# Feed-forward layer 1 by Strassen-Winograd block products, with low halves formed on GpSimd, in a fused two-layer attention kernel

## What is computed

```python
xn3 = _ln(x, g3, be3)                                   # 4096 tokens x 512
ff = jax.nn.relu(xn3 @ Wf1 + bf1) @ Wf2 + bf2           # Wf1 512 x 2048, Wf2 2048 x 512
return x + ff
# layer 1 then needs, per token row, x @ (folded Wt, Wg) + gb, a softmax over tokens,
# a sigmoid gate, and a layer norm
```

## Time and profile before

| | |
|---|---|
| median of 3 runs | 2268.39 us (2266.43 to 2272.82) |
| the profiled execution | 2266.88 us, of which its span is 2265.1 us |
| mean granted TensorE clock | 0.986 |
| busy, share of the span | PE 95%, PE weight load 71%, DVE 60%, ACT 42%, POOL 37% |
| chain that ended last | PE 83%, DVE 7%, ACT 5%, issue 2%, DMA 2%, POOL 1% |
| DMA | 177.35 MB, mean 78 GB/s |

### The profile page before, as it was taken

The page is one execution under the profiler, slowest core; times in us unless marked ns, Lnnn a source line. Parts: engine busy times, 40 slices in busy tenths (PEclk is TensorE's granted clock), DMA queues, the critical chain, the costliest instruction groups (busy, mean ns, idle before and its releaser), DMA issues.

```text
span 2265.1 us, 32190 instructions
## 1 busy us (share of the span) xinstructions
PE 2160.6 (95%) x11590; PEld 1602.6 (71%) x11590; DVE 1356.7 (60%) x3277; ACT 942.5 (42%) x1738; POOL 848.5 (37%) x887
## 2 busy tenths in 40 slices
PE   7999999999999998889999998999999999999996
PEld 5666666666656664467777776888887887888784
DVE  5577766776786667456666676442345536454536
ACT  4155655655565555534433344422322322232223
POOL 1068767777777778653333331000000000000002
PEclk9999999999999998899999999999999999999998
DMA  7655555565564455211111221320111221111101
GB/s 235 78 82 96 95 83 86 102 92 81 91 117 78 77 96 131 71 56 57 57 61 67 84 80 43 121 79 29 61 61 66 70 75 61 66 61 65 43 29 51
DMA packets 106324, 177.35 MB, mean 78 GB/s; under 512 B 18334, under 2 KB 23454, under 8 KB 106160
## 3 DMA queue, kind: packets, MB, share of 16 engines
q1 hardware_dynamic: 106164, 175.29, 33.6%
HBM read 83.67 MB, written 40.13 MB: 55 GB/s over the span
## 4 chain that ended last, share of the span: by engine, by line
PE 83%; DVE 7%; ACT 5%; issue 2%; DMA 2%; POOL 1%; SPq 0%; POOLq 0%; ACTq 0%; DVEq 0%
PE psum L55 20%; PE psum L56 19%; PE psum L57 19%; PE psum L830 6%; PE psum L775 6%; PE psum L818 5%; PE psum L733 1%; DVE psum L1036 1%; PE psum L839 1%; ACT sx L1386 1%; PE psum L1336 1%; PE psum L752 1%; DMA small<-es 1%; PE psum L1328 1%; PE psum L1277 1%
## 5 line engine op out<-in xcount | busy, mean ns | idle before, releaser
L690 POOL TENSOR_TENSOR es<-es,er 128x512 f32<-128x512 f32 (+3 forms) x640 | 587.5, 959 | 258.0 <-PE psum L830 242.9
L931 ACT ACTIVATE er<-psum 128x512 f32<-128x512 f32 (+3 forms) x640 | 278.4, 471 | 285.7 <-DVE psum L1047 178.5
L1036 DVE CUSTOM_DVE_ANT_0 psum<-psum,mask_ts 128x384 f32<-128x384 f32 (+3 forms) x512 | 249.0, 501 | 152.7 <-PE psum L775 150.3
L775 PE MATMUL psum<-ks,qs 96*128 96x512 f32 (+3 forms) x768 | 259.6, 370 | 7.2 <-DVE mx L1036 3.1
L818 PE MATMUL psum<-qs,ks 100*128 100x512 f32 (+3 forms) x768 | 251.3, 364 | 10.7 <-DVE mx L1036 5.4
L1874 ACT ACTIVATE fy<-psum,cols 128x512 f32<-128x512 f32 x128 | 88.2, 689 | 404.9 <-PE psum L57 404.3
L1982 DVE TENSOR_TENSOR hl<-fy,hh 128x512 fp32r<-128x512 f32 x128 | 89.5, 700 | 272.9 <-PE psum L57 195.2
L775 PEld LDWEIGHTS psum<-ks,qs 96*128 96x128 f32 x768 | 139.3, 190 | 115.4 <-issue 32.7
L1040 DVE TENSOR_REDUCE mx<-psum 128x1 fp32r<-128x512 f32 x256 | 175.4, 685 | 61.2 <-PE psum L775 60.3
L55 PE MATMUL psum<-fh,hh 128*128 128x512 f32 x512 | 201.0, 393 | 3.8 <-DVE hl L1982 3.5
L55 PE MATMUL psum<-fah,fh 128*128 128x512 f32 x512 | 203.2, 397 | 0.0
(11 more groups left out here) (260 smaller groups left out, 4539.3 us busy)
## 6 DMA issues: line engine op xcount, KB each, us to landing
qs<-stage SPq DMA_DIRECT2D x96, 256.0 KB, 5.7
ks<-stage SPq DMA_DIRECT2D x96, 256.0 KB, 8.3
rs<-rs_d SPq DMA_DIRECT2D x32, 256.0 KB
sa_d<-rs SPq DMA_DIRECT2D x32, 256.0 KB, 2.1
sx<-sa_d SPq DMA_DIRECT2D x8, 1024.0 KB, 5.8
xt<-in_x SPq DMA_DIRECT2D x32, 256.0 KB, 6.0
x_d<-xt SPq DMA_DIRECT2D x32, 256.0 KB, 2.0
fw<-in_Wf SPq DMA_DIRECT2D x16, 512.0 KB, 5.3
```

The source lines that it names most:

```text
L690: e.tensor_tensor(es, es, er, ALU.add).then_inc(s_add.sem, 1)
L775: t = e.matmul(bank1(*s)[:, v * wd:v * wd + wd], Q.qs[par][0:96, i, 128 * ti:128 * ti + 128], Q.ks[par][0:96, i, c0:c0 + wd], start=True, ...
L931: e.activation(dst, bank1("sc", g, c2, j, i)[:, off:512], ACT.Exp, scale=SCALE).then_inc(s_freeS.sem, 1)
L1036: t = e.tensor_tensor_reduce(out=ps, in0=ps, in1=mask_ts[:, 512 - wd:512], scale=1.0, scalar=-3e38, op0=ALU.add, op1=ALU.max, accum_out=mx ...
```

## The change

The first layer's product for two hidden tiles (256 units) and a chunk of 512 tokens is a 2x2 block product: the weights as a11, a12, a21, a22 (128 units x 256 inputs), the turned rows as b11 to b22 (256 inputs x 256 tokens). Instead of eight block products it forms seven, after Strassen and Winograd. A chunk is 8 such blocks `u`.

- Step `P(c, u, j)`, j = 0 to 6, replaces two `h` steps: 2 contraction blocks x 3 = 6 matmuls with 256 moving columns, so 42 a block, into four half-used banks A, B, C, D. `cp` (ACT) copies product 0 to SBUF (`cu`), and seven `pd` (DVE, 128x256, one operand in PSUM each) combine the products. Tile 2u is complete in bank A after `pd` 3, tile 2u+1 in bank D after `pd` 6.
- Sums of the turned rows: `tt`, four 128x512 subtractions on POOL. High halves of the seven right operands: `bh` (ACT, 7 a chunk); low halves `bl` (DVE, 7 a chunk, two SBUF operands). They replace the 4 copies and 4 subtractions of `cTl`.
- Sums of the weights, once, in chunk 0: `ws`, four 128x256 steps on POOL a block; `wa` 3 high halves on ACT, `wl` 3 low halves on DVE. `wo` writes the block of seven (high and low, 1.8 MB) to DRAM, and from chunk 1 on `wi` reads it back each time, 56 loads into three rotating buffers.
- `hs`, the low half of the relu output, moves from DVE to POOL. Its buffer `fy` is now single (`fr`), `hh` and `hl` have three buffers instead of two.
- The order: a block of TensorE work is 15 slots, `oPPoPPoPPoooPoo`; `o` is split by token tile, and the tiles of block u are consumed in block u+1. All nominal times of the stage are new. Before the seam's end only block 0's seven products stand, where three `h` stood.

```diff
+SLOTS = "oPPoPPoPPoooPoo"
+ADDED_AT = ((1, 2.66), (3, 1.23), (3, 2.65), (5, 1.02), (5, 0.38), (6, 1.29), (6, 1.32))
+HALVES_AT = ((5, 1.55, 2.54, 1.87), (6, 2.6, 2.4, 3.25))
...
+FF_ROWS = (-9.3, -6.31, -3.49, -7.61, -6.54, -5.7)
+FF_TURN = (-2, 0.07, 0.16, 0.01)
+FF_COMBINE = -3.32
...
+            elif s[0] == "wi":
+                n = s[1]
+                u = n % 8
+                w.wait_ge(s_prod, 7 * (n - 2))
...
+                e.dma_start(F.w1[n % 3][:].rearrange("p r a k n -> p (r a k n)").bitcast(F32), w1_d[u]).then_inc(d_wi[n % 3].sem, 16)
...
+            elif s[0] == "hs":
+                _, c, m = s
+                n = 16 * c + m
+                w.wait_ge(s_r3, n + 1)
+                w.wait_ge(s_hh3, n + 1)
...
+                e.tensor_tensor(F.hl[n % 3][:], F.yb[:], F.hh[n % 3][:].bitcast(F32), ALU.subtract).then_inc(s_h3.sem, 1)
+            elif s[0] == "tt":
+                c = s[1]
...
+                w.wait_ge(s_y3, 4 * c + 4)
+                e.tensor_tensor(t1, b12, b11, ALU.subtract).then_inc(s_tt.sem, 1)
+                w.wait_ge(s_tt, 4 * c + 1)
+                e.tensor_tensor(t2, b22, t1, ALU.subtract).then_inc(s_tt.sem, 1)
+                e.tensor_tensor(t3, b22, b12, ALU.subtract).then_inc(s_tt.sem, 1)
+                w.wait_ge(s_tt, 4 * c + 2)
+                e.tensor_tensor(t4, b21, t2, ALU.subtract).then_inc(s_tt.sem, 1)
...
-            elif s[0] == "h":
...
+            elif s[0] == "P":
...
+                wh, wl = (F.w1[n % 3][:, r, LEFT[j]] for r in range(2))
+                for k in range(2):
+                    t = three(e, bk, (wh[:, k, :], wl[:, k, :]), (F.bh[:, j, k, :], F.bl[:, j, k, :]), k == 0, k == 1)
+                t.then_inc(s_prod.sem, 1)
...
+            elif s[0] == "bl":
+                _, c, j = s
+                w.wait_ge(s_bh, 7 * c + j + 1)
+                e.tensor_tensor(F.bl[:, j], quarter(c, RIGHT[j]), F.bh[:, j].bitcast(F32), ALU.subtract).then_inc(s_x3.sem, 1)
+            elif s[0] == "pd":
...
+                w.wait_ge(s_prod, 7 * n + (2, 4, 4, 6, 6, 7, 7)[q])
+                w.wait_ge(s_pd, 7 * n + (0, 0, 2, 3, 3, 3, 5)[q])
...
+                e.tensor_tensor(o, x, y, ALU.add).then_inc(s_pd.sem, 1)
```

More of the change, by code:

```diff
@@ L289, in pre3 @@
     for k in range(KT):
[L290 to L304, removed]
@@ L305 @@
-FF_ROUTE = (35.7, 0, 0.1, 1.3, 1.5, 1.8, 3, 0.2)
-FF_LAST = (3.3, 3.6, -1.2)
-FF_TILE = (0, 0.2, 0.4, 0.8, 0.85, 1, 1.4, 1.6)
-def order3():
-    rows, turn, gate = FF_ROWS, FF_TURN, FF_GATE
-    t = [(n - 2.2 + a, (s, n)) for n in range(4, 16) for a, s in ((-0.01, "wd"), (0, "w"))] + [(15, ("w4",)), (1.81, ("wv",))]
+        t += [(FIRST_TURN[0] + FIRST_TURN[1] * k + a, (s, 0, k)) for a, s in ((0, "cT"), (FIRST_TURN[2], "cTh"))]
+    t.append((FIRST_TURN[3], ("tt", 0)))
+    for j in range(7):
+        a = FIRST_HALVES[0] + FIRST_HALVES[1] * j
+        t += [(a, ("bh", 0, j)), (a + FIRST_HALVES[2], ("bl", 0, j))]
@@ new lines @@
+FF_TILE = (0.05, 0.12, 0.4, 0.8, 1.02, 1.27, 1.86, 1.77)
+FF_WEIGHT = (-3.13, -2.44, -2.12, -1.61, -0.9, -2.72, -0.21)
+FF_END = 2.44
+def order3():
+    rows, turn, ready, slot = FF_ROWS, FF_TURN, FF_WEIGHT, BLOCK / 15
+    t = [(15, ("w4",)), (1.81, ("wv",))]
+    for u in range(8):
+        B = BLOCK * u
+        t += [(B + ready[0], ("wd", 2 * u)), (B + ready[5], ("wd", 2 * u + 1)), (B + ready[6], ("w", 2 * u + 1))]
+        t += [(B + a, (s, u)) for a, s in zip(ready[1:5], ("ws", "wa", "wl", "wo"))]
+    for n in range(8, 64):
+        t.append((BLOCK * (n - 2) + 0.05, ("wi", n)))
@@ new lines, in program @@
+            F.w1 = [block3(0)]
+            F.jk = sb(ctx, "jk", [128, C])
+            F.w2 += [half3(2), half3(3)]
+            with ExitStack() as early:
+                y0 = sb(early, "fy0", [128, KT, 512])
+            F.hh = [sb(ctx, f"hh{p}", [128, 512], F32R) for p in range(3)]
+            F.hl = [sb(ctx, f"hl{p}", [128, 512], F32R) for p in range(3)]
+            F.bh, F.bl = (sb(ctx, f"fa{j}", [128, 7, 2, 256], F32R) for j in "hl")
+            F.xt = [sb(ctx, "fx1", [128, 4, C])]
+            F.w1.append(block3(1))
@@ new lines, in program @@
+            F.wvb = sb(ctx, "wvb", [128, C])
+            F.w1.append(block3(2))
+            F.gb = sb(ctx, "gb", [128, C])
+            F.w2 += [half3(u) for u in range(4, 8)]
+            xn1 = sb(ctx, "fn", [128, 4, C])
+            F.xt.insert(0, sb(ctx, "fx0", [128, 4, C]))
+            with ExitStack() as early:
+                y1 = sb(early, "fy1", [128, KT, 512])
+            F.th, F.tl = [sb(ctx, f"th{i}", [128, KT, 128], F32R) for i in range(2)], [sb(ctx, f"tl{i}", [128, KT, 128], F32R) for i in range(2)]
@@ L1813, in pe3 @@
+                if m == 0 and c:
+                    w.wait_ge(s_o3, 4 * (c - 1) + i + 1)
+                elif m == 0 and i == 0:
+                    w.wait_ge(s_sub, 32)
+                elif m == 0:
+                    freeT(w, tail + i - 1)
+                r = slice(128 * i, 128 * i + 128)
+                three(e, acc[i], (F.hh[p][:, r], F.hl[p][:, r]), (f2h[:, m % 2, :], f2l[:, m % 2, :]),
+                      m == 0, m == 15).then_inc(s_out3.sem, 1)
             elif s[0] == "gT":
```

390 lines of the change are left out of this document (248 added, 142 removed).

## The result

The changed kernel takes 2354.33 us (median of 4 runs, 2349.65 to 2358.05) beside 2270.61 us for the kernel before on the same chip: ratio 1.0367, 95% interval 1.0348 to 1.0386. The prediction said 2262, range 2240 to 2284. The profiled execution has a span of 2356.3 us and a mean granted clock of 0.969 (0.986 before).

A forecast was written before the change was run, and what follows sets the result against it. TensorE was taken as the bound: matmul count times interval, plus waits. -25.2 - 6 + 18.8 + 3 + 2 + 2 = -5.4 us on the median 2268.4 gave 2263, put at 2262 for overlapping stalls; range 2240 to 2284.

The forecast's parts named there:

- The products: Feed-forward on TensorE: seven narrower products a block take 5.00 us instead of 5.44, a gain of 25.2 us (23 to 28).
- The old waits: TensorE's 7.4 us of waits before `gT` and `o` steps should mostly go: a gain of 6 us (0 to 7.4).
- The chain of tile 2u: From product 5 to the next block's first `o`: 3.40 us needed of 4.11, slack 0.71; no wait in a plain block.
- Rival 3: Slower, chance 0.23: tile 2u's low half misses its slot; 2281 us if in a third of the blocks, 2290 in half.
- The move of `hs` to POOL costs nothing by engine shares: 128 `hs` steps go to idle POOL: free by engine shares, but not by the port lock shared with DVE.
- Block 6: Chunks 0 to 6: `bx` on DVE and `tt` on POOL take turns, delaying `pd`; a loss of 18.8 us (0 to 28).
- `bl` at 1.5 us: Sign to look for: DVE's low halves `bl`, like `bx`, lengthened to 1.5 us beside `tt` and `hs` on POOL.
- The `e` steps: Blocks 3 to 5: they can hold `hs` by one DVE step, 0.7 us; a loss of 2 us (0 to 8).
- Block 7: DVE nearly full, `pd` 3 about 1.3 us late: 0.6 us in 5 chunks, a loss of 3 us (0 to 10).
- Chunk 0: Weight sums `ws`, `wa`, `wl` come beside all else, POOL at 5.5 us a block: a loss of 2 us (0 to 8).
- The seam: Between the last cross-attention groups and the feed-forward: DVE gains and loses steps; net 0 us (-3 to +4).
- `wi`: Reading 1.8 MB of weights a block takes some 8 us against 21 us allowed; loads queued behind it cost 0 (up to 5).

## Why the prediction was wrong

**The products: right.** The interval came out at 0.118 us, and where nothing waits (chunk 1 with `bx` away) eight blocks are 3.4 us shorter, 0.43 each where 0.44 was predicted. The gain of 25.2 us was there.

**The old waits: right in part.** No wait before `gT` in the changed kernel; before `gm` it has 2.5 and 1.5 us that the prediction didn't have.

**The chain of tile 2u: right.** Its parts have the predicted lengths, and a plain block shows no wait. At its own upper ends the chain sums to 4.12 us, just over the 4.11 that it has, and four `bx` take 2.6 us by the earlier trace rows and not 2.4; neither changes the outcome. Rival 3, slower through this chain, was the wrong mechanism for the right sign.

**"The move of `hs` to POOL costs nothing by engine shares": the step that failed.** The prediction asked how long `hs` takes on POOL and whom it meets on the port, not what else stands in POOL's queue with it. The reductions stood there, and the trace of before shows the change of kind behind `r5` at 1621.8; it lay inside an idle time of POOL that ended with DVE's next input, so no list of waits named it. A low half that the next `o` needs in 4 us can't stand behind a change that takes 8. The term left out is worth 49 us by the run without reductions, more than all the losses in the sum together (25.8 us). The range missed it wholly.

**Block 6: right in place and mechanism, somewhat small.** Predicted 18.8 us from one stall a chunk of 2.4 to 3.0. Measured were gaps between starts of 2.1 to 3.9 us at that place in all seven chunks, 22.6 us in sum, and moving `bx` away gave 26 (31 for shortening `tt`, which helps the seam too). What exceeds the stalls fits the stretched intervals behind them, which the prediction had for no stall. `bl` at 1.5 us, which it named as a sign, didn't come: 0.74.

**The `e` steps: in the place predicted, larger.** Predicted 2 us (0 to 8) from blocks 3 to 5. At block 6 of chunks 2 to 5 the changed kernel waits 1.7, 2.9, 1.1 and 1.8 us, some 6.5 us more than plain intervals. That the `e` steps make them wasn't tried by itself.

**Block 7: smaller.** Predicted 3 us. The first `o` of block 0 of the next chunk waits 0.74 and 0.72 us, in two chunks, and 0.76 and 0.75 with `bx` away.

**Chunk 0: too small.** Predicted 2 us, at most 8. It became 12.3 us longer instead of 3.5 shorter. `hs` on DVE gave back 5.8 us of that, `bx` away 2.0. Product 6.0, whose bank waits for `cTh` on ACT behind `wa`, stood 3.7 us late in the changed kernel and 2.0 with `hs` on DVE. With `hs` on DVE and `bx` away it took 89.8 us. What makes the rest wasn't tried.

**The seam: wrong.** Predicted -3 to +4, measured +10.7. Block 0's products stand in the first of three gaps, where three wait 1.7, 2.7 and 1.6 us for `bl` (a wait that the prediction had named as a sign of its fall), and the two last groups, without an `h` between them, follow at 11.7 us where they had 9.9 and 8.4 (PE's timeline, starts of the PV products of groups 29 to 31 and the waits behind them):

```profile
1402.37 1.09 PE L1382 MATMUL psum<-pT,vb 128*64 128x128 f32 x16 [1.88 <-DVE xt L1573]
...
1414.00 1.09 PE L1382 MATMUL psum<-pT,vb 128*64 128x128 f32 x16 [0.74 <-ACT pT L1459]
1418.75 0.79 PE L55 MATMUL psum<-W2h,ch 128*128 128x512 f32 x1 [3.66 <-DVE cl L1566]
1425.74 1.09 PE L1382 MATMUL psum<-pT,vb 128*64 128x128 f32 x16 [0.74 <-ACT pT L1459]
```

In that interval `wa` of block 1 on ACT and `wl` on DVE stand in front of `ch` and `cl` (DVE's timeline, L2122 is `wl`):

```profile
1414.59 1.02 DVE L2122 TENSOR_TENSOR fb<-fw,fb 128x512 fp32r<-128x512 f32 x2
1415.74 1.22 DVE L2122 TENSOR_TENSOR fb<-fs,fb 128x1024 fp32r<-128x1024 f32 x1
1416.88 1.21 DVE L1558 TENSOR_REDUCE small<-pp 128x16 f32<-128x1024 f32 x1
1418.01 0.68 DVE L1566 TENSOR_TENSOR cl<-psum,ch 128x512 fp32r<-128x512 f32 x1
```

The prediction had called the last `h` "free filling" and taken its loss as nothing. What the loss is worth wasn't run by itself; the work that came instead isn't free on DVE. 3.8 us of the 10.7 came back by order; the other 6.9 us stay open.

**`wi`: right within its ends.** PE never waited for it. But loads of `e1` issued behind it land up to 9.0 us after their issue, and DVE waited 29.8 us in all for them, in eight places. Two reached PE, the waits of 2.5 and 1.5 us before `gm`, inside the prediction's "0 (up to 5)".

**The clock: left out.** A stall was priced at its own length. Behind the long ones the granted clock was near 0.6 for some 4 us, and stretched intervals account for 26 us of the whole.

## What to carry to other kernels

Before a step is moved to an engine because that engine is idle, list everything that the engine does around it, by kind of instruction: on GpSimd, in this kernel, a reduction over partitions and an ordinary instruction have 6 to 9 us of standing still between them, invisible as long as nobody waits. Keep steps with a short deadline off it near such a change (here: on DVE for 34 of 128 tiles), and keep DVE steps with two SBUF operands out of the places where GpSimd has several steps in a row. And a stall on TensorE costs more than its length, so the stalls of a new order have to be found one by one before its saving is counted.

## What the runs showed of the hardware

- Changing between a reduction over partitions and an ordinary instruction costs GpSimd 5.7 to 9.5 us in the changed kernel (into a reduction 5.7 to 9.5, out of it 7.2 to 9.5); two maxima in a row are 0.30 us apart. MODIFY_POOL_CONFIG stands right behind the last step of the old kind, in the kernel before 41 us ahead of the reduction, which then waited for DVE alone: a lull there hides the cost.
- A DVE addition with two SBUF operands beside a stream of GpSimd additions took 1.57 us instead of 0.68 to 0.73, and GpSimd's 1.62 to 1.74 instead of 1.29. A pair of them so takes some 1.6 to 1.7 us, less than the 1.97 of both lengths alone. The prediction had this from the earlier trace rows; that it held to a tenth of a microsecond in another place was not expected. The Trainium skill, "SBUF — State Buffer", section "SBUF: two separate sides", has the rule, an exclusive lock that each holds for its whole instruction. The trace agrees with it in both places as to who waits for whom, but by the recorded lengths the turns overlap by some 0.3 us.
- After a wait of 9 us the granted clock was 0.59 from 1680 to 1684, then 1.00 from 1684 to 1688.
- The same program ahead of the change reached group 25 between 1337.3 and 1346.1 us in the profiled executions of these kernels. Starts are best compared from a common landmark. Even then, one order of the seam gave 88.3 and 91.9 us, at granted clocks of 0.90 and 0.87.
